# A rounding step of the FFN's activation quantizer moved from VectorE to ScalarE, as two passes

## What is computed

```python
x = x + 0.5 * ffn(layernorm(x), Wf)
x = x + attn(layernorm(x), Wl, Wr, conv, Wa, Wi, Wo, ...)   # gated linear recurrence
x = x + 0.5 * ffn(layernorm(x), Wf)

def ffn(x, weight):
    alpha = max(mean(abs(weight)), EPS)
    w_q = clip(round(weight / alpha), -1, 1)
    beta = max(max(abs(x), axis=-1) / 127, EPS)
    x_q = clip(round(x / beta), -127, 127)
    return (x_q @ w_q.T) * alpha * beta
```

## Time and profile before

| what | value |
|---|---|
| median of 3 runs | 3438.33 us |
| lowest and highest | 3433.92 and 3668.28 us |
| the profiled execution | 3425.26 us |
| its span, slowest core | 3423.7 us |
| spans of the 8 cores | 3405.6 to 3423.7 us |
| TensorE (PE) busy | 2214.0 us, 65% |
| VectorE (DVE) busy | 1184.3 us, 35% |
| ScalarE (ACT) busy | 810.6 us, 24% |
| mean granted TensorE clock | 0.864 |

### The profile page before, as it was taken

How to read it: one execution, slowest core, us unless ns; L and a number is a source line. 1 busy time by engine, 2 the same in 40 slices (tenths; PEclk the granted TensorE clock), 3 DMA queues, 4 the chain that set the end, 5 groups by cost and what they waited for, 6 DMA issues and landing times.

```text
span 3423.7 us, 28756 instructions; the slowest of 8 cores (3405.6 to 3423.7 us)
## 1 busy us (share of the span) xinstructions
PE 2214.0 (65%) x9734; PEld 962.8 (28%) x9734; DVE 1184.3 (35%) x1586; ACT 810.6 (24%) x849; POOL 130.7 (4%) x161
## 2 busy tenths in 40 slices
PE   0015444445079979992999999982797765454445
PEld 0002121112034434441444444430332222222112
DVE  3665444444000005551344444441110025433443
ACT  0653222232011213330343434340000011111110
POOL 0000000000000000000000000000000000000000
PEclk9997777777589989996999999996998886778778
DMA  5631112110724242407354444526424350111111
GB/s 146 243 112 65 62 70 77 75 62 37 153 58 84 65 71 62 86 38 172 56 68 71 65 74 64 76 40 180 108 87 104 99 189 27 49 74 68 56 50 49
DMA packets 252880, 290.34 MB, mean 85 GB/s; under 512 B 168257, under 2 KB 209217, under 8 KB 240449
## 3 DMA queue, kind: packets, MB, share of 16 engines
q0 software_dynamic: 147120, 119.55, 18.6%
q1 hardware_dynamic: 81762, 135.40, 12.2%
q10 hardware_dynamic: 23856, 33.56, 3.1%
HBM read 239.19 MB, written 98.57 MB: 99 GB/s over the span
## 4 chain that ended last, share of the span: by engine, by line
PE 56%; DMA 13%; DVE 13%; ACT 8%; issue 7%; another core or an unknown queue 2%; DVEq 1%; ACTq 0%; SPq 0%; POOLq 0%; POOL 0%
PE pmm L865 10%; PE pmm L874 10%; PE pmm L580 9%; PE pmm L943 8%; PE pmm L751 8%; PE pmm L803 7%; DMA bigA<-s_zn 2%; DMA s_zn<-stg 2%; PE pmm L949 2%; ACT stg L455 2%; PE ptrb L555 2%; DVE stt L451 2%; DVE stt L448 2%; DMA wg<-Wo 2%
## 5 line engine op out<-in xcount | busy, mean ns | idle before, releaser
L580 PE MATMUL pmm<-bigA,wg 128*128 128x512 bf16 x2048 | 512.4, 413 | 496.8 <-DVE bigB L598 248.5
L580 PEld LDWEIGHTS pmm<-bigA,wg 128*128 128x128 bf16 x2048 | 210.2, 105 | 775.1 <-issue 583.4
L865 PE MATMUL pmm<-bigA,wg 128*128 128x512 bf16 x1600 | 360.1, 380 | 62.9 <-DMA bigA<-s_u 62.1
L943 PE MATMUL pmm<-wg,bigA 128*128 128x512 bf16 x1280 | 295.4, 387 | 139.0 <-DMA wg<-Wo 139.0
L874 PE MATMUL pmm<-bigA,wg 128*128 128x512 bf16 x1600 | 358.4, 379 | 0.0
L751 PE MATMUL pmm<-bigA,wg 128*128 128x512 bf16 x1280 | 279.1, 382 | 108.2 <-DMA bigA<-s_zn 108.2
L823 DVE SCALAR_TENSOR_TENSOR sc<-sc,vecs 128x2048 f32<-128x2048 f32 x60 | 141.1, 2351 | 527.3 <-ACT sc L817 523.1
L455 ACT ACTIVATE stg<-bigB 128x2048 bf16<-128x2048 f32 x32 | 61.1, 1909 | 1025.2 <-DVE stt L451 956.7
L803 PE MATMUL pmm<-bigA,wg 128*128 128x512 bf16 x1280 | 280.8, 381 | 21.6 <-DMA wg<-Wr 19.1
L555 PE MATMUL ptrb<-identb,wg 128*128 128x128 bf16 x512 | 105.5, 225 | 266.4 <-DVE wg L539 133.7
L865 PEld LDWEIGHTS pmm<-bigA,wg 128*128 128x128 bf16 x1600 | 156.9, 98 | 253.4 <-issue 66.2
(11 more groups left out here) (123 smaller groups left out, 1708.5 us busy)
## 6 DMA issues: line engine op xcount, KB each, us to landing
bigB<-WfT SPq DMA_DIRECT2D x32, 1024.0 KB, 5.4
bigB<-xN SPq DMA_DIRECT2D x16, 1024.0 KB, 9.1
bigB<-s_x SPq DMA_DIRECT2D x16, 1024.0 KB, 7.1
s_x<-bigB POOLq DMA_DIRECT2D x7, 2048.0 KB, 7.8
out<-bigB POOLq DMA_DIRECT2D x7, 2048.0 KB, 6.8
wg<-Wa POOLq DMA_DIRECT2D x20, 640.0 KB, 9.0
wg<-Wi POOLq DMA_DIRECT2D x20, 640.0 KB, 7.3
wg<-Wl POOLq DMA_DIRECT2D x5, 2048.0 KB, 17.9
```

The costliest lines, as they stand in the source:

```text
L580: e.matmul(p.t[:], wg[:, xof + i * TB + tb * 128: xof + i * TB + tb * 128 + 128], bigA[:, i * D + os * 512: i * D + (os + 1) * 512], start ...
L865: E.pe(lambda e, off=off, c=c, pr=pr, k=k: e.matmul(pr.t[:], wg[:, off:off + 128], bigA[:, c * T + k * TT: c * T + (k + 1) * TT], start=(c ...
L943: E.pe(lambda e, c=c, tb=tb, p=p: e.matmul(p.t[:], bigA[:, c * T + tb * 128: c * T + tb * 128 + 128], wg[:, c * 512:(c + 1) * 512], start= ...
```

## The change

In the loop over the two halves at the end of `pre_mm`, the one VectorE instruction that adds and subtracts C32 becomes two ScalarE passes, the first adding C32 by a bias column, the second adding -C32 in place. Both columns exist already for the weights. Nothing else is changed; from here on lines of the changed kernel are 3 higher than those of the kernel before (L535 becomes L538, L539 becomes L542, L598 becomes L601).

```diff
                     ab = sc[3] if po == 0 else sc[0]
                     at = sc3 if po == 0 else sc0
-                    E.dve(lambda e, zt=zt, at=at: e.tensor_scalar(
-                        at[:, 0:D], zt[:, 0:D], C32, -C32, ALU.add, ALU.add),
-                        reads=[zb], writes=[ab])
+                    E.act(lambda e, zt=zt, at=at: e.activation(
+                        out=at[:, 0:D], in_=zt[:, 0:D], func=AF.Identity,
+                        bias=g0b[:]), reads=[zb, g0_b], writes=[ab])
+                    E.act(lambda e, at=at: e.activation(
+                        out=at[:, 0:D], in_=at[:, 0:D], func=AF.Identity,
+                        bias=c32n[:]), reads=[ab, c32n_b], writes=[ab])
                     E.dve(lambda e, zt=zt: e.tensor_scalar(
                         zt[:, 0:D], zt[:, 0:D], C64, -C64, ALU.add, ALU.add),
                         reads=[zb], writes=[zb])
```

## The result

The changed kernel takes 3483.46 us in the median of 8 runs, the kernel before, run beside it, 3435.65 us. The ratio is 1.014, with a 95% interval of 1.0126 to 1.0154: about 48 us slower, and within 2%. The forecast was 3482.2 us, that is +46.1. In some executions of every kernel one die shows a lower granted clock and the time is longer (up to 3846.21 us here); the two medians include them, every ratio and interval in this document leaves them out. The profiled execution took 3483.35 us, the spans of its cores are 3459.0 to 3481.8 us.

A forecast was written before the change was run, and what follows sets the result against it. It took the uncovered preparations, a strict relay between ScalarE and VectorE while TensorE idles, as the bound: 16 x 2.88 = 46.1 us on a level of 3436.1 gives 3482.2 us, range 3460 to 3505.

The forecast's parts named there:

- The place: All 16 preparations (`pre_mm`), 7 + 7 + 2 over both FFN phases, are waited for, so each one's growth counts.
- The relay: Chain in each preparation from the first L525 to the first PSUM emptying (L598): 12.06 to 14.94 us, +2.88 a round.
- VectorE's relief: Two L532 fewer on VectorE per preparation, 2.68 us a round, spent waiting for ScalarE.
- Rival 1 (relief pays): In the preparations ScalarE's passes hide and VectorE's saving counts: 42.9 us saved, 3393.2 us; chance 0.02.
- The point from which it decides: Old start of the last L539, 9.79 us after L525; six passes fit only at 1.63 us each, rows show 2.0.
- Rival 2 (full overlap): ScalarE's added passes in the preparations follow at the independent 1.91 us: +33.9 us, 3470.0 us; chance 0.06.
- Rival 3 (the clock): TensorE's granted clock changes the rounds' matmul runs, -30.1 to +15.4 us: 3452.1 to 3497.6 us; chance 0.05 at one end.
- the second fall of the clock: In most rounds TensorE's clock falls again after small transposes; it can come or not, costed at nothing.
- Rival 4 (table loads): ScalarE loads a function table for each added pair, 1283 ns each: +87.1 us, 3523.2 us; chance 0.02.
- TensorE's waits: TensorE's waits for L598 and L613, 248.5 and 226.3 us before, should grow 7 x 2.88 = 20.2 us each.

The follow-up runs named there:

- The second FFN alone: The change made only in the second FFN, against the kernel before: 3465.35 us, ratio 1.0079.
- second-half kernel: Against the kernel before, both scalings first, then ScalarE's add and subtract for the second half only; VectorE rounds the first: 3428.73 us, ratio 0.9963.
- interleaved kernel: Changed kernel with ScalarE's passes reordered: both scalings, both adds, both subtracts; VectorE's order kept: 3499.91 us, ratio 1.0181 to the kernel before.
- both queues changed: The interleaved kernel with VectorE also reordered, both C64 steps before both combinations: 3484.42 us, ratio 1.013 to the kernel before.

## Why the prediction was right

- **The place.** The second FFN alone has half the loss, and the kernel with no C32 step gets back 16 rounds' worth. The timings would hardly tell 16 preparations from 14; that the two first ones are on the path too is shown by the traces, where the first matmul of each phase comes 3.2 and 2.9 us later.
- **The relay.** Forecast 14.94 us, measured 14.89 in the round shown and 14.90 in the mean; +2.88 forecast, +2.84 measured. The duration and the pitch taken from the quantizer's L386 and L389 held: the new L532 and L535 take 2.00 us, and dependent passes follow at 2.09. The second scaling to its add pass was the largest small miss, 2.17 instead of 2.19.
- **VectorE's relief.** Forecast as worthless, since VectorE would wait: it does, in front of all four instructions. But it is worth 42.7 us where ScalarE is not asked for anything, and half of it, 1.34 us a round, can be had by giving ScalarE one pair only, behind both scalings. The loss of the changed kernel is the sum of two large terms: -42.7 for VectorE and +88 for ScalarE's passes.
- **Rival 1 (relief pays)** fell here for the reason given: six passes do not fit before VectorE wants the last. The point from which it decides was right: in the second-half kernel four passes take 8.27 us, VectorE wants the result at 8.45, and the sign turns.
- **Rival 2 (full overlap)** fell: its relay would have been 11.91 + 2.27 = 14.18 us and is 14.90, and the added passes stand 2.09 apart. The Trainium skill, "ScalarE: Activation LUTs", section "What ACT_TABLE_LOAD costs", with its overlap of 93 ns for back-to-back ACTIVATEs, is right for passes whose input is complete (1.89 to 1.91 here) and does not hold for a pass that needs the one just before.
- **Rival 3 (the clock)** was costed at nothing with ends of -30 and +15. The four groups, where it acts, grew by 5.5 here and by -3.4 to +10.6 over the kernels: inside the ends, and the second largest term after the relay. The reason given for nothing, that TensorE is cold after 37 us of idling and after 40, speaks of the first of the four runs only; for the second fall of the clock the forecast had none. So it is partly luck that the timing came within 2 us of the forecast: the stretches of the profiled execution add up to +50.8.
- **Rival 4 (table loads)** did not happen: passes follow L525 at 2.19 us, with no room for 1283 ns.
- **TensorE's waits** grew by 22.2 and 22.5 us, not 20.2 each. A wait begins when TensorE's last matmul ends, in the mean of the cores 14.8 and 15.0 us after the eighth emptying before and 14.4 and 14.8 in the changed kernel. TensorE began to wait 0.4 and 0.2 us a round sooner, which is about the size of the extra 2 us in each phase and no part of the relay. Why that end moved has no run of its own.

## What to carry to other kernels

Before moving work to an idle engine, write down the relay instruction by instruction: when each piece is ready, and what is queued in front of whoever wants it, on both engines. Idle time is usable only for work that ends before its consumer would have got there; here one pair of passes cost 29 us placed before the second scaling and gained 13 us placed behind it. An order that suits one engine's queue must be carried into the other's: the same six passes, interleaved, cost 62 us or 45 depending on VectorE's order alone.

## What the runs showed of the hardware

**A wait for an own result that was already complete cost nothing; one for the pass just before cost 0.2 us.** In the interleaved kernel the add and subtract passes also wait for ScalarE's own semaphore, but for a result one pass further back. Each pair takes 3.88 us, and the second pass starts 1.89 us after the first, as passes with no wait do (1.91). In the changed kernel the dependent pass follows at 2.09. So the cost goes with a result that is not complete yet, not with the wait instruction itself.

**The same matmuls took different times in different rounds.** In the two interleaved kernels, whose TensorE code is the same, a round's four runs of 16 matmuls are, in the chain of waits (both queues changed, core 7, then VectorE's queue not changed, core 6):

```profile
565.59 6.18 PE pmm L588 x16
574.89 4.88 PE pmm L588 x16
583.21 3.45 PE pmm L588 x16
589.69 3.45 PE pmm L588 x16
```

```profile
573.76 5.01 PE pmm L586 x16
581.75 3.45 PE pmm L586 x16
588.64 3.45 PE pmm L586 x16
595.12 3.45 PE pmm L586 x16
```

That is 17.96 against 15.36 us. (Core 7's lower mean clock in this execution comes from the second FFN, 0.72 against 0.76 on core 0; in the first FFN, where this round lies, it is 0.77 against 0.78.) Inside the run that took 4.88, the granted clock was still 0.50 (1.2 GHz) a microsecond after its start and 1.00 (2.4 GHz) later:

```profile
575.00:576.00 1.00, 1.00 (x4) 0.34 (x3) 0.89 (x3) 0.00 (x0) 0.00 (x0) 0.50 0.00 0
...
578.00:579.00 1.00, 1.00 (x7) 0.43 (x5) 0.00 (x0) 0.00 (x0) 0.00 (x0) 1.00 0.00 0
```

(us, then busy time of PE, PEld, DVE, ACT, POOL, then the granted clock, DMA share and GB/s.) Ahead of it TensorE had done a stretch of small transposes with pauses between. The same transposes stand ahead of the run that took 3.45 at 581.75 in the other kernel, and there the clock was full:

```profile
582.00:584.00 2.00, 2.00 (x11) 0.92 (x10) 0.81 (x3) 0.72 (x2) 0.00 (x0) 1.00 0.04 8
```

The length of the four groups goes with the time that TensorE spends in them at the lower level. From the mean granted clock of each stretch, over the 14 rounds and in the mean of cores 0 to 3, that is 103.5 us in the kernel with no C32 step, 109.2 in the kernel before, 119.5 in the changed kernel and 125.8 in the interleaved kernel with both queues; the four groups took 425.2, 427.8, 433.5 and 436.5 us. So it moved kernels by up to 11 us against each other, about what one small edit is worth here, and within one kernel the cores scatter as much (421.0 to 432.5 in the kernel before). What decides in a given round whether the clock falls again is not shown: no run moved the start of a round by itself.
